# The reciprocals of a pair of heads are spread by two transfers of 64 partitions each, in place of one of 128

## The reference

```python
x = x + _layernorm(attn(_layernorm(x)))      # q, k normalised per head, softmax, values, projection
x = x + _layernorm(ffn(_layernorm(x)))       # silu gate, two gelu layers of 1024, back to 256

# inside attn, per image b and head h:
sim  = einsum('bhid,bhjd->bhij', l2norm(q) * exp(scale), l2norm(k))
attn = softmax(sim, axis=-1)
out  = einsum('bhij,bhjd->bhid', attn, v)
```

## Time and profile before

| | |
|---|---|
| median of 3 runs | 1941.38 us (1938.71 to 1944.3) |
| the profiled execution | 1939.09 us |
| its span | 1937.2 us |
| PE busy | 1743.2 us, 90% |
| DVE busy | 1203.1 us, 62% |
| ACT busy | 1012.1 us, 52% |

### The profile page before, as it was taken

One profiled execution on the slowest core, in us unless ns is written; L12 is line 12 of the kernel. 1 busy time (PEld: TensorE's weight loads), 2 busy tenths in 40 slices (PEclk: granted clock), 3 DMA queues, 4 the chain that ended last, 5 costly groups with the idle time before them and its releaser, 6 DMA issues.

```text
span 1937.2 us, 24570 instructions
## 1 busy us (share of the span) xinstructions
PE 1743.2 (90%) x8584; PEld 1443.8 (75%) x8584; DVE 1203.1 (62%) x2085; ACT 1012.1 (52%) x1349; POOL 426.7 (22%) x499
## 2 busy tenths in 40 slices
PE   4899899999899889989988984699999999999997
PEld 3677777778678778777777773587878778777876
DVE  4676786786686776776776765664443544444453
ACT  2776676777677667767766763213232331313231
POOL 3333423423323423333333320000000000000000
PEclk8999999999999999999999997799999999999999
DMA  3534544535435445455344355310000000000000
GB/s 117 120 83 116 120 98 115 115 98 121 110 100 121 109 106 132 107 116 129 87 115 111 80 137 132 112 60 2 23 2 23 14 13 23 2 23 2 24 2 22
DMA packets 71445, 152.03 MB, mean 78 GB/s; under 512 B 25968, under 2 KB 26224, under 8 KB 71280
## 3 DMA queue, kind: packets, MB, share of 16 engines
q1 hardware_dynamic: 63504, 122.34, 27.0%
q10 hardware_dynamic: 6624, 23.21, 3.8%
q0 software_dynamic: 1152, 4.19, 0.5%
HBM read 56.91 MB, written 20.19 MB: 40 GB/s over the span
## 4 chain that ended last, share of the span: by engine, by line
PE 51%; DMA 22%; DVE 12%; issue 7%; SPq 4%; ACT 2%; POOL 1%; DVEq 0%; ACTq 0%; POOLq 0%
DMA work<-rows 13%; PE pair L1087 12%; PE pair L1088 12%; PE bank L1009 6%; DMA Dp<-work 5%; PE bank L1023 4%; PE bank L951 4%; DMA rows<-Rp 3%; DVE Pl L675 3%; PE pair L1078 3%; PE pair L1079 2%; DVE work L691 2%; SPq L252 2%; SPq L251 2%; PE bank L1116 2%
## 5 line engine op out<-in xcount | busy, mean ns | idle before, releaser
L1009 PE MATMUL bank<-Ph,V 128*128 128x512 f32 x1024 | 379.9, 412 | 103.3 <-DVE Pl L675 102.9
L1087 PE MATMUL pair<-hh,f 128*128 128x512 f32 x1024 | 405.6, 396 | 18.1 <-DVE hl L787 9.9
L468 ACT ACTIVATE P<-pair,sh 128x1024 f32<-128x1024 f32 x256 | 286.4, 1119 | 246.3 <-PE pair L993 135.6
L1088 PE MATMUL pair<-hl,f 128*128 128x512 f32 x1024 | 404.1, 395 | 0.0
L1009 PEld LDWEIGHTS bank<-Ph,V 128*128 128x128 f32 x1024 | 198.7, 194 | 176.8 <-issue 131.6
L675 DVE TENSOR_TENSOR Pl<-P,Ph 128x1024 fp32r<-128x1024 f32 x256 | 311.9, 1218 | 1.0
L513 ACT ACTIVATE hr<-pair,ct 128x512 f32<-128x512 f32 x128 | 88.2, 689 | 378.8 <-PE pair L1088 378.8
L473 ACT ACTIVATE Ph<-P 128x1024 fp32r<-128x1024 f32 x256 | 271.6, 1061 | 8.1
L1087 PEld LDWEIGHTS pair<-hh,f 128*128 128x128 f32 x1024 | 195.7, 191 | 63.3 <-issue 12.8
L1088 PEld LDWEIGHTS pair<-hl,f 128*128 128x128 f32 x1024 | 195.7, 191 | 41.3 <-issue 0.6
L358 POOL TENSOR_TENSOR rs<-ss,half 128x8 f32<-128x8 f32 x128 | 214.3, 1674 | 10.7
(11 more groups left out here) (101 smaller groups left out, 2852.2 us busy)
## 6 DMA issues: line engine op xcount, KB each, us to landing
stack<-turned SPq DMA_DIRECT2D x128, 384.0 KB, 4.5
stack<-turned SPq DMA_DIRECT2D x128, 256.0 KB, 5.1
work<-rows SPq DMA_DIRECT2D x64, 256.0 KB
f<-raw ACTq DMA_DIRECT2D x22, 512.0 KB, 4.9
raw<-in_h ACTq DMA_DIRECT2D x16, 512.0 KB, 5.3
xt<-in_x SPq DMA_DIRECT2D x8, 512.0 KB, 8.6
xr<-in_x SPq DMA_DIRECT2D x8, 512.0 KB, 8.8
x<-xr SPq DMA_DIRECT2D x8, 512.0 KB, 3.0
```

What stands on the lines that cost most here:

```text
L468: e.activation(M.P[:, i % 2, :], M.SB[i % 2][:, :], ACT.Exp, bias=M.sh[:, h:h + 1]).then_inc(S["exp"])
L1009: d = e.matmul(M.OB[:, :], v, p[:, u % 3, j * 512:(j + 1) * 512], start=jt == 0 and m == 0, stop=jt == 3 and m == 2)
L1087: e.matmul(ps, w, M.hh[src][:, k, :].bitcast(to), start=k == 0, stop=False)
L1088: d = e.matmul(ps, w, M.hl[src][:, k, :].bitcast(to), start=False, stop=k == KH - 1)
```

## The change

`spread_rec` issues two transfers in place of one. Each copies one head's half of the row (512 numbers) to the 64 partitions of that head, and each adds to a semaphore of its own. `normal` waits for its own head's semaphore. The bytes are the same: 128 rows of 2 KB.

```diff
--- before.py
+++ after.py
@@ -267,8 +267,10 @@
     def spread_rec(n):
         q.wait_ge(f"rw{n % 2}", 16 * (n // 2 + 1))
         q.wait_ge("on", 2 * (n - 1))
-        row = M.rows[n].rearrange("(o a) b -> o (a b)", o=2).unsqueeze(1).to_broadcast([2, 64, 512])
-        e.dma_start(M.Rb[:, n % 2, :], row).then_inc(S[f"rb{n % 2}"], 16)
+        for odd in range(2):
+            row = M.rows[n][64 * odd:64 * odd + 64, :].rearrange("a b -> (a b)").unsqueeze(0)
+            e.dma_start(M.Rb[64 * odd:64 * odd + 64, n % 2, :], row.to_broadcast([64, 512])
+                        ).then_inc(S[f"rb{n % 2}{odd}"], 16)
 
     def load_xr(b):
         q.wait_ge("x1", 16 * b)
@@ -686,7 +688,7 @@
         q.wait_ge("nl", n - 1)
         for odd in range(2):
             own = slice(64 * odd, 64 * odd + 64)
-            q.wait_ge(f"rb{n % 2}", 16 * (n // 2 + 1))
+            q.wait_ge(f"rb{n % 2}{odd}", 16 * (n // 2 + 1))
             q.wait_ge("ev", 2 * n + odd + 1)
             e.tensor_tensor(M.on[own, n % 2, :], M.Ev[own, (2 * n + odd) % 4, :], M.Rb[own, n % 2, :],
                             ALU.mult).then_inc(S["on"])
```

## The result

The changed kernel takes 1858.45 us (median of 4 runs, 1853.36 to 1861.81) against 1940.05 us for the kernel before on the same chip: a ratio of 0.9576, 95% interval 0.9544 to 0.9608. 1860 us was forecast.

The account below looks back on a forecast made before the run. PE was taken as the engine with most work, held up by the late copy `work<-rows`. Savings of 63 + 15 + 3 = 81 us from 1939.1 gave 1858, as a median 1860 us; range 1836 to 1891.

Parts of the forecast that it names:

- What bounds it, and the wait: PE has the most work; DVE's waits for the copy `work<-rows` ahead of multiplication L691, 69.6 us, hold it up.
- 25 "issue" waits: Waits of DVE ahead of L691 that the view calls "issue", 39.8 us, claimed to be waits for the copy too.
- Two engines because 2 stands outermost: The old copy, 2 x 64 x 512, runs on 2 DMA engines by its outermost dimension; each new one on 16.
- The new latency: Copy from issue to use: 4.1 us (3.8 to 8.5) against 8.0, some 4 us less on every pair.
- The advice of the same page of the Trainium skill against two halves: Rival: halves serialize on the same engines, the second issued 0.53 us later; 15 us slower, about 1957 us; chance 3%.
- The shared row of DRAM: Rival: packets slow when 16 engines read the same 2 KB; copy takes 5.5 us, kernel 1891 us; chance 12%.
- The second issue is free: One more SP row of 0.53 us, 64 times, lies in slack; without slack it would cost 34 us.
- Term one: Waits at the multiplication, 69.6 us, end except for 6 us in the last slots: 63 us won.
- The 6 us: Wait expected to stay in the last slots: 3.4 us at pair 61 and as much in a second slot.
- Term two: PE's granted clock, at its lower level after long stalls, recovers with the stalls gone: 15 us won (5 to 25).
- the seven windows: Places after long stalls with mean granted clock 0.50 to 0.66, 30 us at half speed; expected near 1 afterwards.
- Term three: `invert` waits 16.7 us for `Dp`, queued behind the copy's packets; some goes, 3 us of it reaching PE (0 to 10).

## Why the prediction was right

*What bounds it, and the wait.* Right. The 25 "issue" waits were waits for the copy: all idle time at the multiplication left with it, 71.7 to 2.5 us.

*Two engines because 2 stands outermost.* Right, by the three kernels that change only this, and by the one with a single transfer. The page's rule on the number of engines ("DMA: Bandwidth & Descriptors" of the Trainium skill, section "Why a DMA increments its semaphore by 16 and not by 1") held at 2, 4, 8 and 16 as far as times, waits and the time of the packets (6.5, 3.2, 2.1, 1.7 us) show it; 16 is told from 8 only weakly. The advice of the same page of the Trainium skill against two halves (section "Rules for kernel authors") held too where the number of engines stays the same: 17 us slower. Here the halves were worth it because the old form left 14 engines idle.

*The new latency.* 4.1 us to use were forecast; the second half landed after some 3.5, and how long DVE then takes to start shows only where it waited. At pair 31 the first packet comes 1.1 us after the issue (1.5 taken) and both halves' packets take 1.5 us of columns (0.5 and about 1 taken). The shared row of DRAM cost little, not nothing: a packet of the copy took 0.088 us in the mean before, 0.092 with the change, and 0.12 in the run where 16 engines read one row 128 times. Nothing of it shows in the kernel's time.

*The second issue is free.* Right, and still right when doubled.

*Term one, 63 us.* PE's idle time fell from 1937.2 - 1743.2 = 194.0 us to 1859.1 - 1729.2 = 129.9, by 64.1; its waits for `Pl` fell by 57.7 of this. They were to fall to some 35 us and stand at 45.2. The 6 us that I left in the last slots were not left at the multiplication, which keeps 0.52 us at pair 60. They stand one step further back, at the inversions of pairs 60 and 61, which wait 4.67 and 3.72 us (2.37 and nothing in the kernel before), by their place in the order for the sums. So the size of what stays was right and its place was not:

```profile
1103.92 0.20 DVE L685 RECIPROCAL Rp<-Dp 128x8 f32<-128x8 f32 x1 [4.67 <-issue]
...
1113.60 1.41 DVE L693 TENSOR_TENSOR work<-work 64x512 f32<-64x512 f32 x2 [0.52 <-DMA work<-rows]
...
1124.64 0.20 DVE L685 RECIPROCAL Rp<-Dp 128x8 f32<-128x8 f32 x1 [3.72 <-issue]
```

*Term two, the clock, 15 us.* PE's busy time for the same matmuls fell from 1743.2 to 1729.2 us, by 14.0, while the mean granted clock rose from 0.966 to 0.980. The figure is good to a few us only: another trace of the same changed kernel has 1726.2. Of the seven windows one is shown above at 1.00; the last slots have 0.91, so not all of the lower level is gone.

*Term three, 3 us, failed as a step.* "Some of this goes", it said of the inversion's waits. They grew by 11 us. That the sums stand behind the `stack` transfers in SP's order is shown by the run that moved them ahead; that DVE, which no longer loses time at the multiplication, reaches the inversion sooner after the sums were asked for is the likely reason for the growth, and not shown. Taking these waits away gained nothing. So the term had the wrong sign for DVE and should have been 0 for the time: 64.1 + 14.0 = 78.1 against the 81 of the sum is that term. That the other two sum so closely is luck in part, since one came out 1.1 us over and the other 1.0 under.

What the prediction missed is of another kind. It charged the old copy for being late, and only 3 us for the engines that it held. The second charge is about 30 us when such a copy runs in the changed kernel. A repair that had only moved the multiplication to a later slot might have left that part of the loss; this was not tried. In the old kernel the `stack` transfers landed at most 0.3 us later than now, so little of the second charge shows there, and how the 78 us divide between the two causes stays open.

## What to carry to other kernels

When a broadcast or gather is late, look at how many DMA engines it uses while it is alone (packets a us, or the share of 16), before anything is split or moved: a small outermost dimension, such as two heads ahead of 64 repeats, can leave most of them idle. Bring a larger dimension to the front (16 here; 8 gave the same time, 4 nearly all of it); whether that makes one transfer or two mattered little here. And a transfer on few engines can cost twice, by its own lateness and by that of later transfers that need a share of the same engines; the second cost may show only once the first is gone.

## What the runs showed of the hardware

- Sixteen engines read one and the same 2 KB of DRAM 128 times, and 256 KB landed in 3.3 us. The packets took 0.12 us each in the mean, where those of the old copy on two engines took 0.088 and those of the change 0.092. Whether the shared row or the longer transfer makes them longer was not tested; the kernel's time does not show it.
- A 128 KB copy landed 2.9 us after issue on 16 engines; a transfer that nobody waits for, on two engines, made others on 16 engines land later (5.6 us for 4.4) and the kernel 30 us slower, while the same bytes on 16 engines cost nothing that shows.
- VectorE, 65% busy, lost 29.3 us of idle time ahead of its inversions (31.1 to 1.8), and neither its idle time as a whole (657 us) nor the kernel's time changed.
